# Causal mask of an attention stage added by VectorE in the instruction that finds a row's maximum

## What is computed

```python
scores = jnp.einsum('bqhd,bkhd->bhqk', xq, xk) * scale
causal_add = jnp.triu(jnp.full((S, S), MASK_NEG, dtype=jnp.float32), k=1)
scores = scores + causal_add[None, None]
probs = jax.nn.softmax(scores, axis=-1)
attn = jnp.einsum('bhqk,bkhd->bqhd', probs, xv).reshape(B, S, q_size)
return attn @ Wo
```

## Time and profile before

| | |
|---|---|
| median of three runs | 896.63 us |
| span of the profiled execution | 899.0 us |
| PE busy | 805.2 us, 90% |
| DVE busy | 646.9 us, 72% |
| ACT busy | 573.7 us, 64% |
| POOL busy | 454.5 us, 51% |

### The profile page before, as it was taken

How to read it: one execution, slowest core, us unless ns; L and a number is a source line. 1 busy time by engine, 2 the same in 40 slices (tenths; PEclk the granted TensorE clock), 3 DMA queues, 4 the chain that set the end, 5 groups by cost and what they waited for, 6 DMA issues and landing times.

```text
span 899.0 us, 16806 instructions
## 1 busy us (share of the span) xinstructions
PE 805.2 (90%) x4840; PEld 680.3 (76%) x4840; DVE 646.9 (72%) x1580; ACT 573.7 (64%) x1538; POOL 454.5 (51%) x410
## 2 busy tenths in 40 slices
PE   3788899799999999999999999999889879899990
PEld 3677678578878888887888887888777668787870
DVE  5855565478887777887978878877579957756573
ACT  3355556677776877776777777677566655555550
POOL 1473504487465775664656655445243684003274
PEclk9999989999999999999999999999899999999995
DMA  9398953211000100010000000000000055257685
GB/s 295 115 292 262 281 143 100 74 16 24 1 1 14 18 14 7 1 17 9 1 13 12 1 1 1 1 2 2 7 1 1 25 201 157 70 150 205 192 245 175
DMA packets 52952, 70.73 MB, mean 79 GB/s; under 512 B 7552, under 2 KB 44672, under 8 KB 52480
## 3 DMA queue, kind: packets, MB, share of 16 engines
q1 hardware_dynamic: 40768, 47.61, 17.2%
q0 software_dynamic: 9216, 16.82, 7.6%
q10 hardware_dynamic: 2880, 5.24, 2.0%
HBM read 42.61 MB, written 27.03 MB: 77 GB/s over the span
## 4 chain that ended last, share of the span: by engine, by line
PE 55%; issue 13%; POOL 13%; DVE 9%; ACT 4%; DMA 3%; POOLq 0%; ACTq 0%; DVEq 0%; SPq 0%
PE ps L1648 45%; PE ps L1846 5%; POOL xs L1558 3%; POOL xs L1565 3%; POOL sb_ropeB L1593 2%; POOL sb_xf L1596 2%; PE ps L1702 2%; POOL sb_x L1584 2%; DVE sb_x L1444 1%; PE ps L1665 1%; POOL sb_wF L1604 1%; POOL sb_wF_raw L1579 1%; PE ps L1716 1%; DVE sb_wF L1424 1%; ACT sb_prob L985 1%
## 5 line engine op out<-in xcount | busy, mean ns | idle before, releaser
L1648 PE MATMUL ps<-sb_wF 128*128 128x512 f32 (+2 forms) x1056 | 280.3, 387 | 15.6 <-DVE sb_wF L1434 5.8
L1648 PEld LDWEIGHTS ps<-sb_wF 128*128 128x128 f32 x1056 | 170.6, 192 | 29.7 <-DVE sb_wF L1424 8.7
L1593 POOL TENSOR_TENSOR sb_ropeB<-sb_ropeB,sb_sin 128x512 f32<-128x512 f32 x80 | 107.7, 1346 | 147.8 <-ACT sb_ropeB L965 147.3
L985 ACT ACTIVATE sb_prob<-ps,sb_nmax 128x128 f32<-128x128 f32 (+3 forms) x256 | 134.4, 526 | 62.9 <-DVE sb_nmax L1417 61.6
L1648 PE MATMUL ps<-sb_wF,sb_wA 128*128 128x512 f32 x576 | 156.0, 406 | 5.9 <-ACT sb_ropeB L965 4.4
L1417 DVE TENSOR_REDUCE sb_nmax<-ps 128x1 f32<-128x128 f32 (+3 forms) x256 | 121.4, 482 | 49.5 <-PE ps L1648 47.7
L1424 DVE TENSOR_TENSOR sb_wF<-ps,sb_wF 128x512 fp32r<-128x512 f32 x160 | 109.2, 683 | 39.2 <-ACT sb_wF L994 38.8
L1604 POOL TENSOR_TENSOR sb_wF<-sb_xf,sb_wF 128x384 fp32r<-128x384 f32 (+1 forms) x75 | 84.0, 1121 | 98.1 <-ACT sb_wF L977 98.0
L1444 DVE SCALAR_TENSOR_TENSOR sb_x<-ps,sb_rinv,sb_x 128x256 f32<-128x256 f32 x256 | 122.4, 478 | 15.6 <-PE ps L1648 6.6
L1648 PEld LDWEIGHTS ps<-sb_wF,sb_wA 128*128 128x128 f32 x576 | 103.2, 191 | 26.8 <-ACT sb_ropeB L965 5.6
L1648 PE MATMUL ps<-sb_wA,sb_wF 128*128 128x256 f32 x768 | 115.6, 287 | 4.1 <-DVE sb_x L1444 2.1
(11 more groups left out here) (203 smaller groups left out, 1322.4 us busy)
## 6 DMA issues: line engine op xcount, KB each, us to landing
ys<-sb_wA_raw SPq DMA_DIRECT2D x124, 128.0 KB, 2.5
sb_wF_raw<-xs SPq DMA_DIRECT2D x44, 128.5 KB, 4.5
sb_wA_raw<-xs SPq DMA_DIRECT2D x44, 128.5 KB, 2.6
sb_work<-xs SPq DMA_DIRECT2D x36, 128.5 KB, 2.7
sb_wA_raw<-in_wattn ACTq DMA_DIRECT2D x18, 256.0 KB, 4.7
sb_wF_raw<-in_wgu SPq DMA_DIRECT2D x4, 768.0 KB, 10.9
sb_wF_raw<-in_wdn SPq DMA_DIRECT2D x4, 768.0 KB, 12.4
sb_wA_raw<-in_wgu SPq DMA_DIRECT2D x4, 768.0 KB, 8.0
```

The lines of the kernel that those rows point to most:

```text
L985: nc.scalar.activation(prob[k % 2][:, h, 0:(i + 1) * P], ps[:, bank_of((k * G + h) % (UB * G)), 0:(i + 1) * P], ACT.Exp, bias=nmax[:, k % ...
L1593: nc.gpsimd.tensor_tensor(ropeB[:, slot], ropeB[:, slot], sin[:], ALU.mult).then_inc(rope_mul, 1)
L1648: return nc.tensor.matmul(out, lhsT, rhs, start=start, stop=stop)
```

## The change

The scores are held negated: `SCALE` becomes negative, so that S leaves minus the scores in PSUM. The mask matmuls are gone, and with them `identb` and `causal`. The mask is now a bf16 table of 128x512 with +2.38e38 above the diagonal, kept in SBUF once for even and once for odd turns, in the unused columns of the slots of `wF`. VectorE's `max` becomes one `tensor_tensor_reduce`: it reads the scores from PSUM and the mask from SBUF, writes the masked, negated scores to `prob` in SBUF, and gives the row's minimum as its accumulator output. `exp` reads and writes `prob` in place with scale -1. S now waits for `nmax_done` in place of `exp_done`, and the wait for `pt_done` moves from ACT to DVE. The mask is loaded twice on SyncE's queue (128 KB each), where `identb` and `causal` were loaded once (32 KB each).

```diff
-    SCALE = float(P) ** -0.5
+    SCALE = -float(P) ** -0.5
+
+    def mask_slots(n):
+
+        at = (EVEN, ODD)[n] + 3
+        return wF_mask[:, at:at + 3:2, 0:2 * P]
+
+    def mask_of(g, i):
+
+        m = mask_slots(g % 2)
+        if i == 0:
+            return m[:, 1:2, P:2 * P]
+        if i == 1:
+            return m[:, 1:2]
+        return m[:, :, (T - 1 - i) * P // 2:2 * P]
...
-        sp.dma_start(identb[:], A["identb"]).then_inc(mask_in, 16)
-        sp.dma_start(causal[:], A["causal"]).then_inc(mask_in, 16)
-        tiles(pools[0], pools[1])
+
+        tiles(pools[0], pools[1], lambda: mask(0), pools[0].ns + 1)
+        mask(1)
...
             act.wait_ge(nmax_done, m + 1)
-            if not (b == 0 and k < 2):
-                act.wait_ge(pt_done, b * PB + tiles_before(k - 1, b))
-            nc.scalar.activation(prob[k % 2][:, h, 0:(i + 1) * P], ps[:, bank_of((k * G + h) % (UB * G)), 0:(i + 1) * P],
-                                 ACT.Exp, bias=nmax[:, k % 2, h:h + 1], accum_out=ssum[:, k % 2, h:h + 1]).then_inc(exp_done, 1)
+            own = prob[k % 2][:, h, 0:(i + 1) * P]
+            nc.scalar.activation(own, own, ACT.Exp, scale=-1.0, bias=nmax[:, k % 2, h:h + 1],
+                                 accum_out=ssum[:, k % 2, h:h + 1]).then_inc(exp_done, 1)
...
             dve.wait_ge(s_done, m + 1)
+            if b == 0 and h == 0 and k in (0, T):
+                dve.wait_ge(mask_in[k // T], 16)
             if not (b == 0 and k < 2):
                 dve.wait_ge(exp_done, m - 2 * G + 1)
-            nc.vector.tensor_reduce(nmax[:, k % 2, h:h + 1], ps[:, bank_of((k * G + h) % (UB * G)), 0:(i + 1) * P],
-                                    AX_X, ALU.max, negate=True).then_inc(nmax_done, 1)
+                dve.wait_ge(pt_done, b * PB + tiles_before(k - 1, b))
+            added = mask_of(k // T, i)
+            parts = added.shape[1]
+            scores = ps[:, bank_of((k * G + h) % (UB * G)), 0:(i + 1) * P].rearrange("p (a c) -> p a c", a=parts)
+            masked = prob[k % 2][:, h, 0:(i + 1) * P].rearrange("p (a c) -> p a c", a=parts)
+            nc.vector.tensor_tensor_reduce(masked, scores, added, 1.0, TOP, ALU.add, ALU.min,
+                                           nmax[:, k % 2, h:h + 1]).then_inc(nmax_done, 1)
...
             if not (b == 0 and m < 3):
-                pe.wait_ge(exp_done, b * UB * G + m - bank_before(m) + 1)
-            elif m == 0:
-                pe.wait_ge(mask_in, 32)
+                pe.wait_ge(nmax_done, b * UB * G + m - bank_before(m) + 1)
...
             if i == 0:
-                mm(o, first_q(g, h), first_k(g), True, False)
+                ins = mm(o, first_q(g, h), first_k(g), True, True)
             else:
                 mm(o, q_at(g, h, 0)[:, rows], k_at(g, 0)[:, 0:(i + 1) * P], True, False)
                 mm(o, q_at(g, h, 0)[:, rows], k_at(g, 1)[:, 0:(i + 1) * P], False, False)
-                mm(o, q_at(g, h, 1)[:, rows], k_at(g, 0)[:, 0:(i + 1) * P], False, False)
-            mm(o[:, rows], identb[:], causal[:], False, True).then_inc(s_done, 1)
+                ins = mm(o, q_at(g, h, 1)[:, rows], k_at(g, 0)[:, 0:(i + 1) * P], False, True)
+            ins.then_inc(s_done, 1)
```

More of the change, by code:

```diff
@@ L16 @@
 EPS = 1e-5
+TOP = 3.4028234e38
 class Pool:
@@ L78, in program @@
         wA_raw = sb("wA_raw", [P, 40, 512], F32, own)
+    with ExitStack() as own:
+        wF_mask = sb("wF_mask", [P, 40, 1024], BF16, own)
     def routing(at, name):
@@ L124, in program @@
     ident = sb("ident", [P, P], F32)
-    identb = sb("identb", [P, P], BF16)
-    causal = sb("causal", [P, P], BF16)
     wgt = sb("wgt", [P, N], F32)
@@ L175, in program @@
     ident_in = sem("ident_in")
-    mask_in = sem("mask_in")
+    mask_in = [sem(f"mask_in{n}") for n in range(2)]
     cf_in = sem("cf_in")
@@ L781, in store_tile, with mask, tiles @@
             sp.dma_start(ys[q.p][s * P:(s + 1) * P, :], yo(at)).then_inc(y_out[at % RING], 16)
-        def tiles(first, second, then=lambda: None):
+        def mask(n):
+            sp.dma_start(mask_slots(n), A["mask"]).then_inc(mask_in[n], 16)
+        def tiles(first, second, then, at):
             loads = [(first, s) for s in range(first.ns)] + [(second, s) for s in range(second.ns)]
@@ L788, in tiles @@
             for m, (q, s) in enumerate(loads):
-                if m == XR:
+                if m == at:
                     then()
@@ L830, in last_constants @@
             rank_constants(pools[3])
-        tiles(pools[2], pools[3], last_constants)
+        tiles(pools[2], pools[3], last_constants, XR)
         for b in range(B - 1):
@@ L1963, in layouts @@
         "ident": np.eye(P, dtype=f),
-        "identb": np.eye(P, dtype=f).astype(bf),
-        "causal": np.triu(np.full((P, P), -2.3819763e38, f), k=1).astype(bf),
+        "mask": np.concatenate([np.zeros((P, 3 * P), f), np.triu(np.full((P, P), 2.3819763e38, f), k=1)], 1)
+                  .reshape(P, 2, 2 * P).astype(bf),
         "cos": np.concatenate([np.cos(ang), np.cos(ang)]).astype(f),
```

## The result

Ten runs of the changed kernel have a median of 890.13 us (886.35 to 892.52), ten of the kernel before beside them 896.74 us (891.89 to 899.58). The ratio is 0.9931, 95% interval 0.9910 to 0.9951: 6 to 7 us, 0.7% faster. 873.6 us were forecast, 23 us less. The sign is right, the size under a third of it.

A forecast was written before the change was run, and what follows sets the result against it. PE was taken to bound ordinary attention turns, busy 35.00 of 35.00 us. Masks gave 30.7 us, less 3 for waits and 5 for six turns: 22.7, rounded to 23, so 896.6 - 23 = 873.6 us; range 864 to 892.

The forecast's parts named there:

- A mask's price: PE in the attention: each of 256 mask matmuls removed saves 0.12 us, 30.7 us in all, bounds 17.9 and 35.8.
- The new VectorE instruction: DVE's `max` with the mask from SBUF: the stream itself is free, about 685 ns at 512 columns.
- The rival of two cycles for an element: DVE's new instruction takes 0.33 us longer per `max`, so the kernel gets 35 us slower, 932 us; chance 0.13.
- The readout: DVE's accumulator after each `max`: 0.1 us of occupancy and delay, bounds 0 and 0.2, 1.6 us a turn.
- exp: ACT's exp reading from SBUF, not PSUM: 0.02 us more each, 0.4 us a turn, which fits.
- The moved waits and the mask's loads: S waiting for the maximum only adds room; `max` waiting for `pt_done` costs nothing; SyncE's two 128 KB loads are hidden.
- What becomes late next: PE's T waiting on exp: 0.2 us a turn, 3 us in all, plus 5 us lost in six turns already waiting.
- At half: Three layer norm turns and three or four last turns, where PE already waits for DVE: 6 x 0.9 = 5 us lost.
- half is lost: DVE's readout nearer 0.2 us makes PE wait before T and V, losing 10 to 14 us: 884 to 888; chance 0.2.
- Nothing: Another engine sets the attention's turn as soon as PE is faster: 892 to 901 us; chance 0.07.

The follow-up runs named there:

- both moves: Reciprocal of tile row 1 behind `x_add2`, layer norm's scaling of two tiles held until DVE's part of J 3: changed kernel 884.08 us, kernel before 892.7 us.
- experiment 10: The kernel before with each mask matmul issued twice, each with half the mask's value: 948.50 us beside 940.94, ratio 1.0071.
- Experiment 4: The changed kernel with S waiting for exp again and DVE writing masked scores back to PSUM, where exp reads them: 889.33 us, ratio 0.9919.
- Experiment 3: The changed kernel with S waiting for exp again, not for the maximum: 888.81 us, ratio 0.9922.
- the first move: DVE's reciprocal of tile row 1 moved behind `x_add2`: changed kernel 886.39 us, ratio 0.9903; kernel before 895.99 us, ratio 0.9995.
- experiment 7: The changed kernel with DVE's reciprocal of tile row 1 moved behind `x_add2`: 886.39 us, ratio 0.9903.
- experiment 1: The kernel before without its 256 mask matmuls, scores left unmasked, nothing else changed: 887.5 us, ratio 0.9904.
- experiments 5 to 8 and 12 to 14: Changed kernel and kernel before: layer norm cut 0.9891, 1.001; reciprocal moved 0.9903, 0.9995; with layer norm scaling held too 0.9849, 0.9962; changed kernel again 0.9937.
- experiments 1 to 4: Kernel before without masks 0.9904; changed kernel with zero matmuls for masks 1.0048, with S waiting for exp 0.9922, and also masked scores in PSUM 0.9919.

## Why the prediction was right or wrong, step by step

**A mask's price: right.** 0.12 us was forecast. With the reciprocal moved, turn 5 has no listed wait of PE. PE in order of time, for the changed kernel with both moves:

```profile
352.17 0.60 PE L1879 MATMUL ps<-sb_ident,sb_prob 128*128 128x128 f32 x4
...
385.32 0.60 PE L1879 MATMUL ps<-sb_ident,sb_prob 128*128 128x128 f32 x4
```

A turn of 33.15 us, where the kernel before has 34.88: 1.73 us for 16 masks, 0.108 us each, 27.7 us for 256. It is the forecast turn (33.0 to 33.3). The slot is 0.05 us (experiment 10). The other 0.06 us are read as the weight load that the mask exposes behind it; the J that takes 0.10 us longer behind a mask fits this, but no run took that load away alone. The Trainium skill, "VectorE: DVE Perf Modes", its section on the TRN2 errata, gives 56 ns for a matmul of 128 columns; experiment 10 agrees for a second mask (0.05 us), and the 0.108 us show that it is not the price of the first.

**The new VectorE instruction: right, its readout too dear.** The stream was to be free: 686 ns against 685. The rival of two cycles for an element falls, and the trace agrees with the rule of the Trainium skill that spoke against it ("DVE: opcode table, instruction layouts, handler registers and perf-mode slots", its section on datapath and trigger behaviour), that a stage that reads its own result has no bubble. The readout was put at 0.1 us of occupancy; it lasts 83 ns, and the next instruction starts at the same time (359.96 us, above), so DVE's busy time in a turn is 27.28 us as before (27.22).

**exp: 0.03 us, not 0.02.** Experiment 4 gave it back and gained nothing measurable.

**The moved waits and the mask's loads: right.** Experiment 3 shows no gain from the bank, and S has no wait. The second expert block kept its length too: from the last transpose to the end it is 129.4 us before and 129.0 us after.

**What becomes late next: wrong, and this is the step that failed.** The prediction took the room of one wait, 0.46 us between exp and T, for that of every turn, and let the turns in which PE already waits keep half of the gain. 8 us were to be lost: 0.2 us a turn, and half of the gain in six turns. 21 us were lost (27.7 - 6.6). By turns, at 1.73 us for 16 masks:

- Turns 0, 1, 2, 6 and 10: forecast 3 x 0.9 us lost, in fact all of 5 x 1.73 and 0.1 more, 8.7 us. "At half" had no row behind it. Where PE already waited, an earlier PE waited longer. Turns 0 and 1 I had not counted at all: the list of waits that I read the earlier trace rows began at 283 us. In turn 0 PE waits 4.4 us in all before and 4.5 changed. In turn 1 it waits 0.3 us in all before and 1.8 us changed, 1.07 us of it for ACT's rope copies:

```profile
218.75 1.65 PE L1675 MATMUL ps<-sb_wF,sb_wA 128*128 128x512 f32 x6 [1.07 <-ACT sb_ropeB L986]
```

- The seven ordinary turns: 12.1 - 8.4 = 3.7 us, 0.5 a turn where 0.2 were forecast. The forecast's room of 0.46 us between exp and T was one of many; the smallest one decides. In turn 4 a part of it is J, which starts as ACT's copy ends (325.71 + 0.59 = 326.30 us), in the changed kernel, all engines:

```profile
325.49 0.87 PE L1675 MATMUL ps<-sb_wA,sb_wF 128*128 128x256 f32 x6
...
325.71 0.59 ACT L986 ACTIVATE sb_ropeB<-ps 64x512 f32<-64x512 f32 x1
...
326.35 0.98 PE L1675 MATMUL ps<-sb_wF,sb_wA 128*128 128x512 f32 x3
```

  This is not in the list of PE's waits, since the gap is short; only the distance from W to J tells it (326.35 - 325.49 = 0.86 us, where 0.71 do in turn 5 with both moves, 358.13 to 358.84). That is 0.15 us; where the other ordinary turns lose theirs was not followed one by one.
- Turns 12 to 15 hold 16, 16, 15 and 11 masks, 6.3 us. 13 to 15 gave 0.8 us and turn 12 next to nothing at an equal clock (below): 5.5 us lost, where "half" meant 3.
- The rest, about 3 us, is in no turn of 0 to 11 or 13 to 15. 0.6 us of it are the six masks ahead of turn 0. For the others, in turn 12 and the expert blocks, TensorE's clock is the candidate (below).

**The rival that came near** was "half is lost", and its time was 884 to 888. Its mechanism, waits of PE that the handmade order makes, is the one that the runs show; its cause, a readout of 0.2 us, is not. It spread its loss evenly over the turns and had none that give nothing. "Nothing", in which another engine sets the turn at once, is near the truth for turns 0, 1, 2, 6, 10 and 12 and false of the seven ordinary ones. The measured 890.1 us lies between the times of these two rivals. That the wide range of 864 to 892 us holds it is no merit of the forecast's mechanism, whose own range was 867 to 880.

**What stays open.** The two moves brought 3 us of the 21 back. Turns 6 and 10 still are 37.6 and 36.9 us where 37.9 and 37.9 stand in the kernel before with the moves, so 1.4 and 0.7 us are missing there. PE's listed waits in turn 6 sum to 1.60 us with the change and both moves and to 1.27 without the change, which explains 0.3 us. Turn 1 gains nothing in any version. The new wait for the rope copies is its largest, and the same with one or both moves; nothing was tried on it. Other orders were not tried.

## What to carry to other kernels

An engine that is busy for a whole stretch is worth speeding up only until the next one is late. Before counting the gain, go through the engine's steps in each kind of turn and write down the smallest room of each wait on another engine; the gain of a turn ends there. Here the turns in which the engine already waited gave nothing, not half. A short list of waits does not say that there is room.

An order written by hand fits the engine speeds for which it was written. When one changes, the steps that are in nobody's hurry (here the layer norm of the next batch) are worth moving behind those for which the faster engine waits: that brought as much as the change itself, 6.6 us, of which the kernel before could have had 3.5.

The price of a small matmul depends on its neighbours. Here taking it out gave 0.11 us, its slot (0.05 us) and what is read as the weight load exposed behind it (0.06 us); a second one added to it cost only the slot.

## What the runs showed of the hardware

**DVE waits for POOL at SBUF.** DVE's instruction on four elements, `TENSOR_TENSOR sb_mv<-sb_stats`, takes 0.17 us where POOL does nothing (at 238.24 us in the kernel before). In turn 5 it takes 0.55 us before, 0.89 us in the changed kernel, and with the move, from this answer of experiment 7, 0.27 us:

```profile
355.26 1.01 POOL L1631 TENSOR_TENSOR sb_wF<-sb_xf,sb_wF 128x384 fp32r<-128x384 f32 x1 [0.88 <-ACT sb_wF L998]
...
356.03 0.27 DVE L1093 TENSOR_TENSOR sb_mv<-sb_stats 128x4 f32<-128x4 f32 x1
```

In all three its end is that of POOL's instruction: 362.84 and 362.82 us, 358.75 and 358.73, 356.30 and 356.27. So most of that time is read as a wait for POOL to end. In the changed kernel POOL still had 0.87 us to go when DVE came, in the kernel before 0.53 us. The Trainium skill, "SBUF — State Buffer", its section on SBUF's two separate sides, says that DVE with two inputs from SBUF and GpSimd share a port pair which one of them holds for its whole instruction; the trace agrees. The new VectorE instruction reads one operand from PSUM, and its 686 ns show no such wait. The forecast looked for this only there, and not at the steps of the layer norm whose place beside POOL would shift.

**TensorE's clock made turn 12 longer or shorter, not the kernel.** Turn 12 as a stretch (start:end, length, busy PE, PEld, DVE, ACT, POOL, granted clock, DMA), in the kernel before with the first move, in that with both, and in the changed kernel with the first and with both:

```profile
606.70:653.20 46.50, 42.33 (x280) 36.11 (x279) 31.31 (x75) 31.98 (x79) 19.35 (x17) 1.00 0.01 4
```

```profile
604.30:652.00 47.70, 43.67 (x279) 37.12 (x278) 31.29 (x75) 31.90 (x79) 19.34 (x17) 0.96 0.01 4
```

```profile
597.10:646.30 49.20, 43.57 (x264) 38.17 (x263) 31.49 (x91) 33.33 (x81) 20.00 (x17) 0.93 0.01 4
```

```profile
596.30:647.10 50.80, 45.15 (x263) 39.61 (x262) 31.48 (x91) 33.32 (x81) 19.98 (x17) 0.90 0.01 4
```

1.00 is 2.4 GHz throughout; below it a part of the stretch ran at 1.2 GHz. The length follows the clock and not the masks: the profiled kernel before has 49.4 us at 0.93, the changed one 47.6 at 0.96 and, run again, 50.7 at 0.90. From 0.96 to 0.90 it is 3 us. At an equal clock the masks make little difference: 49.4 us with them and 49.2 in the changed kernel (48.4 in experiment 1) at 0.93, 47.7 and 47.6 at 0.96. So turn 12 gave next to nothing back. In the profiled kernel before the clock falls in this stretch:

```profile
632.00:646.00 14.00, 11.68 (x52) 9.02 (x51) 5.79 (x15) 7.79 (x18) 5.24 (x5) 0.76 0.03 9
```

It begins with a wait of PE, busy for 1.68 of the 4 us from 632 to 636, where the routing stands in its order; from 636 to 640 the granted clock is 0.50, and behind 646 us it is 1.00 again.

Over all runs on one chip (experiments 5 to 8 and 12 to 14) the mean granted clock was 0.9766 for the kernel before (45 runs) and 0.970 for the changed one (12 runs). Among these runs of the kernel before, a time regressed on the clock gives 4.1 us for 0.01 (standard error 1.3, correlation 0.45). So 0.007 less would be some 3 us, an estimate, about what the turns leave over. But the 17 runs of the kernel before on another chip (experiments 1 to 4) show no such slope. The changed kernel, in which PE waits more, was granted less. No experiment held the clock fixed, so this is argued, not shown.
